# A two-layer transformer block: 20 spare transposes in place of 135 at the beginning

## The reference

```python
mod = (_silu(L0_c) @ L0_wmod).reshape(L0_c.shape[0], 6, 1, -1)
h = _layernorm(x, axis=-1) * (1 + ca) + sa
x = x + ga * _L0_attn_ref(h, ...)      # 16 heads of 16, softmax within blocks of 64 tokens
h = _layernorm(x, axis=-1) * (1 + cb) + sb
x = x + gb * _L0_ffn_ref(h, ...)       # three cycles of a small coupling network with gelu
...                                    # layer 1, with modulation of its own:
x = x + ga * _L1_attn_ref(h, ...)      # 8 heads of 64, causal, with a look-ahead term
x = x + gb * _L1_ffn_ref(h, ...)       # 8 experts, each takes its top 128 tokens of a batch
```

## Time and profile before

| | us |
|---|---|
| median of 3 runs | 1887.47 (1887.31 to 1887.69) |
| profiled execution, its own time | 1887.51 |
| its span | 1886.3 |
| TensorE busy in the span | 1867.0 (99%) |
| DVE, ACT, POOL busy | 1069.4, 904.7, 684.4 |
| TensorE's granted clock, mean over the span | 0.999 |

### The profile page before, as it was taken

One profiled execution on the slowest core, in us unless ns is written; L12 is line 12 of the kernel. 1 busy time (PEld: TensorE's weight loads), 2 busy tenths in 40 slices (PEclk: granted clock), 3 DMA queues, 4 the chain that ended last, 5 costly groups with the idle time before them and its releaser, 6 DMA issues.

```text
span 1886.3 us, 30943 instructions
## 1 busy us (share of the span) xinstructions
PE 1867.0 (99%) x11545; PEld 1295.8 (69%) x11545; DVE 1069.4 (57%) x2840; ACT 904.7 (48%) x1918; POOL 684.4 (36%) x771
## 2 busy tenths in 40 slices
PE   8999999999999999999999999999999999999998
PEld 6756566656665666666566655656777888888887
DVE  7777675567557655846675564577534456232221
ACT  4756665565556555654654675454445221111111
POOL 3213344324332433433243333344444333333332
PEclk9999999999999999999999999999999999999999
DMA  4200010001000100100010000031130233233333
GB/s 134 80 26 1 12 40 2 23 1 40 1 23 2 40 13 12 40 2 23 1 40 12 12 1 15 34 127 53 43 81 12 79 89 80 38 78 87 79 82 69
DMA packets 59715, 76.82 MB, mean 41 GB/s; under 512 B 7128, under 2 KB 52848, under 8 KB 59312
## 3 DMA queue, kind: packets, MB, share of 16 engines
q1 hardware_dynamic: 46464, 57.28, 9.1%
q0 software_dynamic: 12288, 16.79, 5.2%
q10 hardware_dynamic: 816, 0.79, 0.1%
HBM read 53.71 MB, written 21.00 MB: 40 GB/s over the span
## 4 chain that ended last, share of the span: by engine, by line
PE 90%; DVE 0%; POOL 0%; issue 0%; ACT 0%; DMA 0%; POOLq 0%; DVEq 0%; ACTq 0%
PE bank L780 14%; PE bank L999 12%; PE bank L1012 11%; PE bank L849 7%; PE bank L904 4%; PE bank L873 4%; PE bank L885 4%; PE bank L797 4%; PE bank L858 3%; PE bank L917 3%; PE bank L765 3%; PE bank L835 2%; PE bank L599 2%; PE bank L727 2%; PE bank L813 1%; PE bank L658 1%
## 5 line engine op out<-in xcount | busy, mean ns | idle before, releaser
L1254 ACT ACTIVATE h<-bank 128x512 f32<-128x512 f32 x128 | 76.0, 597 | 340.5 <-PE bank L999 336.2
L999 PE MATMUL bank<-xin,ew 128*128 128x256 f32 x1024 | 235.0, 382 | 0.0
L1012 PE MATMUL bank<-ew,h 128*128 128x256 f32 x1024 | 226.5, 379 | 0.0
L1807 POOL TENSOR_TENSOR s<-s,ri 128x256 f32<-128x256 f32 (+3 forms) x128 | 160.1, 1263 | 182.6 <-DVE ri L1557 182.2
L1012 PEld LDWEIGHTS bank<-ew,h 128*128 128x128 f32 x1024 | 194.6, 190 | 26.7 <-issue 0.6
L999 PEld LDWEIGHTS bank<-xin,ew 128*128 128x128 f32 x1024 | 189.6, 190 | 25.7 <-issue 2.8
L1845 POOL DMA_INDIRECT out<-y,indices x64 | 102.2, 1597 | 286.9 <-DVE y L1694 195.3
L1230 ACT ACTIVATE s<-s,mn 128x128 f32<-128x128 f32 (+3 forms) x256 | 140.9, 551 | 101.2 <-DVE mn L1550 100.4
L1535 DVE SCALAR_TENSOR_TENSOR th<-th,bank 128x384 f32<-128x384 f32 (+1 forms) x192 | 104.1, 594 | 120.7 <-ACT th L1221 120.7
L1694 DVE SCALAR_TENSOR_TENSOR y<-bank,gates,gbe 128x256 f32<-128x256 f32 x64 | 31.0, 484 | 248.2 <-PE bank L1012 248.1
L1564 DVE COPY pT<-bank 128x384 f32<-128x384 f32 (+1 forms) x192 | 106.0, 594 | 84.4 <-PE bank L885 84.3
(11 more groups left out here) (322 smaller groups left out, 3513.5 us busy)
## 6 DMA issues: line engine op xcount, KB each, us to landing
ew<-L_ffn_w SPq DMA_DIRECT2D x24, 1024.0 KB
x1s<-x_scratch SPq DMA_DIRECT2D x8, 512.0 KB
out<-x1s SPq DMA_DIRECT2D x8, 512.0 KB, 2.9
xn_scratch<-n_xn SPq DMA_DIRECT2D x8, 512.0 KB, 2.9
x<-L_attn_x SPq DMA_DIRECT2D x7, 512.0 KB, 3.8
x_scratch<-x SPq DMA_DIRECT2D x7, 512.0 KB, 3.0
wqkv<-w_qkv SPq DMA_DIRECT2D x1, 3072.0 KB, 10.0
wqkv<-L_wmod SPq DMA_DIRECT2D x2, 1024.0 KB, 6.6
```

What stands on the lines that cost most here:

```text
L999: mm = te.matmul(banks[i][:, g * 2 * P:(g + 1) * 2 * P], w1[:, kk, (2 * n + g) * P:(2 * n + g + 1) * P], xin[:, kk, :, :].rearrange("p h s ...
L1012: mm = te.matmul(banks[i][:, 0:D], ex.h1[:, g, n * P:(n + 1) * P], w2[:, g, :], start=(g == 0), stop=(g == FC - 1))
L1807: done = g.tensor_tensor(sc, sc, b1.ri[u % 2][:, m, :].unsqueeze(2).to_broadcast([P, 2, w]), ALU.mult)
```

## The change

```diff
-SPARE = (17, 3, 5, 8, 13, 13, 15, 10, 7, 4, 5, 25, 10)
+SPARE = (8, 1, 1, 1, 1, 1, 1, 1, 1, 1, 1, 1, 1)
```

## The result

| | before | after |
|---|---|---|
| median, us (13 runs each) | 1887.47 | 1893.55 |
| lowest to highest | 1887.20 to 1887.95 | 1890.61 to 1896.23 |
| ratio, 95% interval | | 1.0032 (1.0023 to 1.0040) |

The account below looks back on a forecast made before the run. TensorE, busy for 1867.0 of 1886.3 us, was taken to bound the kernel; falls of the clock behind three rests, 1.3 + 1.65 + 1.65, less 0.15 gained, gave +4.4 us on 1887.47: 1891.9 us, range 1887.1 to 1896.5.

Parts of the forecast that it names:

- the three places that I named: Rests near 9 us, at 91 to 94.5 and at 117.4 to 122.98, each followed by a fall of the clock.
- No group holds up what follows it; the gains are 0.15 us: At every cut group the next step waits for something else; gains of 0.1 and 0.05 us, against 13.2 at most.
- Rests of 1.9, 3.6, 2.6 and 1.3 us: TensorE idle for these times near 9, 91, 118 and 122 us once the spares are gone.
- 1.65 us for each fall: Cost of each clock fall, taken between nothing and 3.3 us lost, before any wait that takes some up.
- First rest, 1.3 us: Near 9 us: 1.65 us less the 0.37 us TensorE waits anyway ahead of the projections at 13.78.
- Second rest, 1.65 us: Behind the 3.6 us rest at 91 us: matmuls from 94.64 on stand in the ACT, DVE, TensorE chain; 1.65 us.
- may come back late: Rival, longer or more falls: clock late in the chain from 94.6 to 99 us, 3.3 us, total +7.75; chance 0.15.
- Third rest, 1.65 us: Behind the rests at 117.4 to 122.98 us: next to no idle from 122.98 on, so 1.65 us in full.
- The spares near 70 us cost nothing: The 8 at 68.81 and 13 at 72.63 us, cut to 1 each: gain 0, no fall counted.
- a fourth fall: Rival, longer or more falls: rests left by 19 spares between 68.8 and 74 us; 1896.9 us; chance 0.15 together.
- Transposes hold the clock, as read from the trace: The clock came up while TensorE did transposes for 2.3 of 3.3 us; matmuls behind 4.37 us of spares ran full pace.
- Times further apart than before: The moment of a fall may differ by execution, so the changed kernel's times should spread beyond the 0.4 us of before.

Follow-up runs that it names:

- cut_cycle: Only the 38 spares between batch 0's first coupling cycle and the next cut to 3, against the kernel before: 1890.90 us, +3.43, ratio 1.0016.
- cut_proj: Only the 35 spares around the third set of transposed rows cut to 2, against the kernel before: 1890.16 us, +2.69, ratio 1.0014.
- The kernel with 83 spares: Against 135 before: start and 68.8 and 72.6 us full, other two long rests half, one each elsewhere: 1887.28 us, ratio 1.0000.
- cut_start: Only the first 20 spares (two groups) cut to 9, against the kernel before: 1888.74 us, +1.27, ratio 1.0007.
- half_70: Against 135 spares before, 75: half at the three long rests, full at 68.8 and 72.6 us, one each elsewhere: 1888.51 us, +1.03.
- cut_70: Only the groups at 68.8 and 72.6 us (8 and 13 spares) cut to 1 each, against the kernel before: 1888.52 us, +1.03, ratio 1.0003.
- the halves made of transposes and of matmuls: Against the kernel before: half the spares at three long rests, one elsewhere, 1888.55 us; same with half as many plain matmuls, 1888.44 us.

## Why the prediction was right

The predicted 1891.9 us stands against 1893.55, +4.4 against +6.1 with an interval that begins at +4.3. The mechanism was right: the rests cost the clock, at the three places that I named (a granted clock of 0.50 for 10.1 us in cut_cycle and 6.7 us in cut_proj; first projections of 851 to 1222 ns instead of 592 in the changed kernel), though at the first it is mostly a late rise and not a fall. By its steps:

- *No group holds up what follows it; the gains are 0.15 us.* Right: the steps behind the cut groups start where they did, relative to their releasers (10.79 against 10.77; 73.84 and 75.76 with the lag of 2.2 taken off are 71.6 and 73.6, the second 0.6 us behind DVE's first piece as at the start), and doubling the counts shows that the waits end where the groups do. The kernel with 83 spares is 0.13 us below the one before.
- *Rests of 1.9, 3.6, 2.6 and 1.3 us.* Measured 1.73, 3.51, 2.42 and 0.85 between matmuls; the single spares and the slow thin transposes shorten them.
- *1.65 us for each fall.* No run shows this term. It was an estimate, half of the 3.3 us of work ahead of the rise at the start; in its place the runs had +3.43 at the second rest and +2.69 at the third, and +1.27 at the first, where 0.37 was taken off. The fall at 1882.9 in the trace of before is there: its granted clock is 0.52 over 1882.9 to 1883.0 and 0.50 over the microsecond behind.
- *First rest, 1.3 us.* cut_start: +1.27. The size holds, but what I described, a rise at 9 us and a fall behind the rest, is not what happened: in that kernel's profile, as in the changed one's, the nine spares are done before 9 us, and the clock rises late, by the durations at about 15 and 17 us. Of the profiles only that of half_70 has the fall, at 12.0. That 1.3 fits 1.27 is partly luck; in the changed kernel's profile the same place costs 2.2.
- *Second rest, 1.65 us.* This is the term that was mis-sized: cut_cycle has +3.43. I took the 3.3 us of work at the start as the time in which the clock comes back. In the chain of waits it stayed down for 10.1 us (13.6 in the changed kernel), and TensorE then became the late one itself, at L707. I had this as "may come back late" in a rival, with 3.3 us.
- *Third rest, 1.65 us.* Mis-sized too: cut_proj has +2.69, with 6.7 us at 0.50; the fall comes before the projections start, and their first 4.0 us all run at that clock.
- *The spares near 70 us cost nothing.* Wrong in half of the executions: cut_70 has +1.03 in the median with a fall at 74 us. I named it as a fourth fall in a rival, but the forecast has it at nothing.
- *Transposes hold the clock, as read from the trace.* Right: cutting transposes alone made the clock fall (to 0.50 in cut_cycle, cut_proj and cut_70), and the medians of the halves made of transposes and of matmuls came out 0.11 us apart.
- *Times further apart than before*: 5.6 us against 0.8.

What I left out would have brought the sum further up, to 1.27 + 3.43 + 2.69 + 1.20 = 8.6, more than the change has. So the predicted sum came near partly by luck: two of its terms are too small by 2.8 us together and a fourth is missing, and the whole loses less than its parts do one by one. In the changed kernel's profile the fourth place loses nothing and the third 1.9 us instead of 2.69; why remains open.

## What to carry to other kernels

An instruction that does nothing useful can be worth its time if it stands in a wait (here 115 fewer of them made the kernel 6.1 us slower): look not only at what removing it frees, but at how long its engine then rests, and at what clock the next stretch is granted. Where the work behind a rest is one chain through several engines, don't count on the waits to hide a fall: in cut_cycle TensorE worked for 8.55 us at a granted clock of 0.50, by estimate (half of them) 4.3 us more than at 1.00, and 3.43 of them reached the end, because the clock came back late and the engine turned into the late one. Fill a wait to the point at which the next step's input is ready and no further: half-filling was enough at two places (0.0 us in ten of eleven runs), not at the start (+1.0), and overfilling cost nearly its full length (+12.1 us for 15.5).

## What the runs showed of the hardware

Two short rests can bring the fall, which my forecast had at nothing. In cut_70 it came behind 1.20 and 0.57 us with over a microsecond of matmuls between (granted clock 0.50 from 74.0 to 77.3 us), while the earlier trace rows have a single one of 1.6 us without harm. The same kernel does it in about half of its executions (six of eleven by their times): the fall isn't tied to a step of the kernel, and a kernel with such rests gets times of two kinds (1887.3 to 1887.5 and 1888.5 to 1888.9). And the clock can stay down for long on a busy engine: 10.1 us at 0.50 in cut_cycle, with TensorE busy for 8.55 of them.
